# Gather passes of a graph layer: the second products of a block are issued behind the first products of the next block

## What is computed

```python
out = x @ root + bias
for r in range(8):
    mask = (edge_type == r)
    sums = segment_sum(x[src] * mask[:, None], dst, num_segments=1250)
    cnt  = segment_sum(mask, dst, num_segments=1250)
    out  = out + (sums / maximum(cnt, 1)[:, None]) @ weight[r]
```

## Time and profile before

| | us |
|---|---|
| median of 3 runs | 2362.14 (2356.88 to 2371.85) |
| the profiled execution | 2366.44 |
| span of its trace | 2364.7 |
| busy TensorE, matmuls | 2077.4 (88%) |
| busy VectorE | 1341.4 (57%) |
| busy ScalarE | 818.3 (35%) |
| busy GpSimd | 917.9 (39%) |
| the first and last product of the gather passes begin | 1064.5 and 1691.1 |

### The profile page before, as it was taken

The page is one execution under the profiler, slowest core; times in us unless marked ns, Lnnn a source line. Parts: engine busy times, 40 slices in busy tenths (PEclk is TensorE's granted clock), DMA queues, the critical chain, the costliest instruction groups (busy, mean ns, idle before and its releaser), DMA issues. The chain is left out here.

```text
span 2364.7 us, 27801 instructions
## 1 busy us (share of the span) xinstructions
PE 2077.4 (88%) x9485; PEld 1623.2 (69%) x9485; DVE 1341.4 (57%) x2374; ACT 818.3 (35%) x1068; POOL 917.9 (39%) x805
## 2 busy tenths in 40 slices
PE   7898988889999999969999999899799379999910
PEld 5676776667888888857767677677588258888810
DVE  7467667652222222209999998988798722222258
ACT  3111111112222222215555566666534123333311
POOL 0000045455555554007777777777300111000034
PEclk9999999999999999989999999999899789999965
DMA  5222265657777777559888898886355679875163
GB/s 172 83 71 71 88 210 180 207 181 258 261 262 254 247 251 265 210 161 319 302 295 293 285 331 292 306 297 230 102 179 174 260 233 332 299 291 211 45 246 118
DMA packets 159197, 524.55 MB, mean 222 GB/s; under 512 B 33578, under 2 KB 33962, under 8 KB 157024
## 3 DMA queue, kind: packets, MB, share of 16 engines
q1 hardware_dynamic: 84752, 313.16, 37.2%
q0 software_dynamic: 70432, 195.65, 25.5%
q10 hardware_dynamic: 3888, 14.16, 1.5%
HBM read 403.66 MB, written 148.94 MB: 234 GB/s over the span
## 5 line engine op out<-in xcount | busy, mean ns | idle before, releaser
L194 PE MATMUL psum<-w_hi,xnT_hi 128*128 128x512 f32 (+1 forms) x1600 | 440.8, 412 | 27.2 <-PEq L401 21.4
L194 PE MATMUL psum<-w_lo,xnT_hi 128*128 128x512 f32 (+1 forms) x1600 | 426.8, 397 | 0.0
L194 PE MATMUL psum<-w_hi,xnT_lo 128*128 128x512 f32 (+1 forms) x1600 | 414.9, 393 | 0.0
L792 POOL DMA_INDIRECT sorted_rows<-acc x313 | 332.9, 1064 | 116.4 <-issue 85.1
L194 PEld LDWEIGHTS psum<-w_hi,xnT_hi 128*128 128x128 f32 (+1 forms) x1600 | 305.2, 194 | 100.6 <-issue 24.7
L194 PEld LDWEIGHTS psum<-w_lo,xnT_hi 128*128 128x128 f32 (+1 forms) x1600 | 301.4, 188 | 75.0
L194 PEld LDWEIGHTS psum<-w_hi,xnT_lo 128*128 128x128 f32 (+1 forms) x1600 | 296.8, 186 | 73.5
L521 ACT ACTIVATE work<-psum 128x512 f32<-128x512 f32 (+1 forms) x150 | 89.9, 599 | 591.2 <-PE psum L194 527.7
L761 DVE TENSOR_TENSOR acc<-acc 128x1024 fp32r<-128x1024 f32 x64 | 78.5, 1227 | 380.0 <-DMA split_experts<-acc 259.3
L884 POOL DMA_INDIRECT w_lo<-y_rows,sort_row x176 | 232.9, 1324 | 92.1 <-issue 58.5
L884 POOL DMA_INDIRECT w_hi<-y_rows,sort_row x176 | 236.4, 1343 | 62.9 <-issue 53.2
(11 more groups left out here) (279 smaller groups left out, 2615.9 us busy)
## 6 DMA issues: line engine op xcount, KB each, us to landing
split_experts<-acc SPq DMA_DIRECT2D x128, 512.0 KB
ring<-split_experts SPq DMA_DIRECT2D x16, 4096.0 KB, 15.0
w_raw<-in_wchunks SPq DMA_DIRECT2D x88, 512.0 KB
y_rows<-work SPq DMA_DIRECT2D x144, 256.0 KB
acc<-in_wchunks SPq DMA_DIRECT2D x64, 512.0 KB
o_rows<-o_s ACTq DMA_DIRECT2D x27, 512.0 KB
work<-local_rows SPq DMA_DIRECT2D x26, 384.0 KB
acc<-in_bias SPq DMA_DIRECT2D x10, 512.0 KB, 9.7
```

What stands on the lines that cost most here:

```text
L194: i = pe.matmul(to[:rm, :], x_[:, k, m * P:m * P + rm], w_[:, s, k * HALF:(k + 1) * HALF], start=(n == 0), stop=(n == 3 * KD - 1))
L792: pool.indirect_dma_start(sorted_dram, IndirectOffsetOnAxis(ap=e_dest[:, c:c + 1], axis=0), e_rec[:, c, :], None, bounds_check=BLOCKS * P ...
```

## The change

TensorE's instructions are the same ones, in another order; no other engine's code changes. Before, a block had its hi products, three matmuls of the unit, then its lo products. Now a block has its hi products, then the lo products (or the direct products) **of the block before**, then three matmuls of the unit. Waits move with the instructions that they stand before: those for the flush and for `hot` of a new group still stand ahead of its first hi products, and now also ahead of the last products of the old group.

```diff
+                def first_part(j):
+                    n, g, k = SPLIT_NO[j], j // GROUP, j % GROUP
+                    pe.wait_ge(hi_done, n + 1)
+                    ...                                   # two hi products
+                    o.then_inc(hi_used, 1)
+
+                def last_part(j):
+                    b, g, k = j % SLOTS, j // GROUP, j % GROUP
+                    if direct(j):
+                        pe.wait_ge(landed[b], PLACED[b] + 16 * (j // SLOTS) + 16)
+                        pe.wait_ge(scaled_done, DIRECT_NO[j] + 1)
+                    else:
+                        pe.wait_ge(lo_done, SPLIT_NO[j] + 1)
+                    ...                                   # two direct or lo products
+                    o.then_inc(pe_done, 1)
...
-                        for j in range(GROUP * g, GROUP * (g + 1)):
-                            if direct(j):
-                                ...                       # three of the unit, then direct products
-                            else:
-                                ...                       # hi products, three of the unit, lo products
+                    for j in range(i * SLOTS, (i + 1) * SLOTS):
+                        g = j // GROUP
+                        if j % GROUP == 0:
+                            if g >= 2:
+                                pe.wait_ge(acc_done, ACC_NO[g - 2])
+                            pe.wait_ge(hot_done, g + 1)
+                        if not direct(j):
+                            first_part(j)
+                        if j >= 1:
+                            last_part(j - 1)
+                        for _ in itertools.islice(steps, 3 * KD // SLOTS):
+                            pass
+                last_part(BLOCKS - 1)
```

More of the change, by code:

```diff
@@ L986, in _ @@
                     pass
+                def first_part(j):
+                    n, g, k = SPLIT_NO[j], j // GROUP, j % GROUP
+                    pe.wait_ge(hi_done, n + 1)
+                    for q in range(2):
+                        o = pe.matmul(bank[2 * (g % 2) + q], hot[:, g % 2, k, :], y_hi[:, n % 2, q * HALF:(q + 1) * HALF],
+                                      start=k == 0, stop=False)
+                    o.then_inc(hi_used, 1)
[6 more added lines that the diff above has]
+                        pe.wait_ge(lo_done, SPLIT_NO[j] + 1)
+                    for q in range(2):
+                        at = slice(q * HALF, (q + 1) * HALF)
+                        if direct(j):
+                            o = pe.matmul(bank[2 * (g % 2) + q], hot_scaled[:, DIRECT_NO[j] % 2, :],
+                                          slot_of(b).bitcast(F32)[:, at], start=k == 0, stop=k == GROUP - 1)
+                        else:
+                            o = pe.matmul(bank[2 * (g % 2) + q], hot[:, g % 2, k, :], slot_of(b)[:, at],
+                                          start=False, stop=k == GROUP - 1)
+                    o.then_inc(pe_done, 1)
@@ L987, in _ @@
                 for i in range(PASSES):
                     steps = unit(UNIT_AT[i]) if i in UNIT_AT else iter(())
[L989 to L993, removed]
-                        for j in range(GROUP * g, GROUP * (g + 1)):
-                            b, k = j % SLOTS, j % GROUP
-                            first, last = k == 0, k == GROUP - 1
-                            if direct(j):
[L998 to L1004, removed]
-                            else:
[L1006 to L1018, removed]
```

## The result

| | before | changed |
|---|---|---|
| median, 8 runs each | 2363.35 (2356.88 to 2371.85) | 2382.18 (2377.88 to 2387.74) |
| profiled execution | 2366.44 | 2377.88 |
| span of its trace | 2364.7 | 2376.1 |

The ratio is 1.0073, with a 95% interval of 1.0054 to 1.0092: 13 to 22 us slower, some 17 by the ratio (the two medians of the table lie 18.8 apart), under the 1% that the prediction called no change. The forecast was 2373, its own range 2366 to 2381, the whole range 2360 to 2385. Direction and range held; the size was 11 us where some 17 came, and the median lies 1 us above the forecast's own range.

What follows compares the result with a forecast made beforehand. TensorE was taken to bound 39 passes at 13.88 us, VectorE the passes without a unit; 7.0 (longer loop in root passes) + 4.0 (passes behind those) = 11.0, 2362.1 + 11.0 = 2373 us; own range 2366 to 2381, whole 2360 to 2385.

Steps and rivals of the forecast that it cites:

- The bound and the loop: Passes with unit and root result: TensorE's 13.88 us gives way to a 14.32 loop, 0.44 longer; 16 x 0.44 = 7.0 us.
- 0.10 after its end. With 0.68 that is 0.78: Pass start: first hi products begin 0.10 us after `hot` ends, which takes 0.68, so 0.78 after its start.
- the cover of 0.35: Passes 22 to 30 and 33 to 41: loop without root result 13.53 us, under TensorE's 13.88, 0.35 to spare, no cost.
- every pass pays: Rival, chance 0.09: cover of 0.35 or the gathers' fails, 18 passes without root results pay too, 2381 to 2389 us.
- The passes behind those without a unit: Passes 10, 21, 32 and 43: direct products stand behind the wait, 4 x 1.0 = 4.0 us, between 0 and 9.8.
- (a): Passes 9, 20, 31, 42: TensorE's order is covered by VectorE's 15.82 of 16.59 us; costed at nothing.
- (b): Lo products and the slot's next gather come 0.47 us later; cover 1.45, costed at nothing.
- (c): Flush behind VectorE's fourth lo part: the direct products it needs are over earlier, cover over 3 us; costed at nothing.
- (d): Hi products released earlier give ScalarE a lead that a TensorE-bound pass can't use; costed at nothing.
- The wait did not dissolve: Rival, chance 0.14: VectorE runs ahead further, `hot` is ready in time at pass starts; 2362 us.
- The clock did not fall: Rival, chance 0.08: gaps in root passes bring half clock to half of some 17 passes, 24 plus 11: 2397 us.
- the 13.9 us: GpSimd contention with VectorE's lo parts: seven of 45 ns in 44 passes would be 13.9 us; left out.

Runs made afterwards that it cites:

- the first experiment: Changed order, but at a pass start the direct products come first again, ahead of the waits for the flush and `hot`: 2360.73 us, ratio 1.0002 to the kernel before.
- the dose of 0.14: Changed order with an extra 128x256 VectorE copy between flush and root result, once per pass with a root result: 2380.22 us, ratio 1.0084 to the kernel before.
- the second experiment: Old order, only the direct products moved behind the next pass's first hi products: 2398.86 us, ratio 1.0155 to the kernel before.
- the first kernel of the last experiment: Changed order with direct products first, one filling matmul per block and two more direct blocks in passes without a unit: 2356.23 us, ratio 0.997 to the kernel before.
- the third experiment: Changed order, but VectorE makes the next pass's first `hot` ahead of adding the root result: 2364.98 us, ratio 1.002 to the kernel before.

## Why the prediction was right, and where its sizes were off

**The bound and the loop held.** The kernel got slower through a longer loop at a pass start, with a cause that stands in one place: the first experiment removes it and loses nothing, the dose of 0.14 comes through as 0.14, the shortened link as 0.33. The signs named ahead were there: waits of 0.46 us ahead of the first hi products, VectorE over a microsecond for ScalarE before the fourth lo part (1.32), ScalarE for the second hi products (1.45), 13.82 to 13.89 in passes 22 to 30 and 33 to 41.

**The loop was mis-sized at two links of five,** by 0.16 and 0.07. Predicted, against the timeline above:

| link | predicted | measured |
|---|---|---|
| start of `hot` to first hi products | 0.78 | 0.94 |
| hi, direct products, unit | 2.88 | 2.95 |
| to the fourth lo part | 1.90 | 1.89 |
| lo part and flush | 1.20 + 1.13 | 1.20 + 1.14 |
| to the next `hot` | 6.43 | 6.43 |
| sum | 14.32 | 14.55 |

The first is the step "0.10 after its end. With 0.68 that is 0.78", which carried the gap of pass 9's second group over to the first group of a pass. Here the products begin 0.25 after the recorded end (1253.55 to 1253.80). The size of the matrix, 128x384 there and 128x512 here, is not the reason. In pass 2 of the changed kernel the same 128x512 matrix is followed after 0.1 us, and the link is the predicted one, 0.79. VectorE, then TensorE, for whose wait the row names no releaser:

```profile
1088.23 0.68 DVE L944 TENSOR_TENSOR hot<-lanes,sort_local 128x512 fp32r<-128x512 f32 x1
```

```profile
1089.02 0.70 PE L991 MATMUL psum<-y_hi,hot 128*128 128x512 f32 x2 [0.31 <-issue]
```

Passes 1 and 2 take 14.38 and 14.39 us, and only from pass 3 on is it 14.53 and more. With `hot` in two pieces the gap behind a piece of 128x128 is likewise 0.10 in passes 1 and 2 and 0.26 from pass 3 on. What the slow starts have in common stands in the code: from unit 4 on, which begins in pass 3, a unit has a wait of its own (for a result to have left its PSUM bank), and TensorE meets it right ahead of the group's waits. In the changed kernel every start on `hot` with that wait ahead comes after 0.25 to 0.26 (passes 3 to 8, 10, 12 to 19, 21, 32), and every one without it after 0.10 (passes 1, 2, 9, 20 and 43, and the second groups for which TensorE waited). The trace of before shows the same 0.25 at pass 21. No experiment moved this wait alone, and why it costs 0.15 is open. The second link is long by the 0.08 of a pair behind a gap: without a gap, in the experiment with the root result behind the next matrix, it took 2.87. Together 0.23 in each pass, so 0.67 instead of 0.44 over 13.88: 10.4 us measured in the 17 root passes with a unit against 7.0 for 16. Without a root result the loop is 14.55 - 0.79 = 13.76, so the cover of 0.35 was 0.12 and just held. The rival "every pass pays" was nearer than its 0.09 says; the second experiment shows the same passes at 14.23 once 0.47 more stands in the loop.

**The passes behind those without a unit** were put at 4.0 with bounds 0 to 9.8. Passes 10, 21 and 32 cost 6.7 and the end 1.5, so 8.2: within the bounds, double the term. Pass 21 alone costs 4.2, over its bound of 2.45. (The forecast's own range doesn't come out of the bounds either: 7.0 with 0 and with 9.8 gives 2369 to 2379, not 2366 to 2381.) The term took the 12.53 us of pass 21 as those of a pass at full clock. From `hot` to `hot` it was one, but the direct products just ahead ran mostly at half clock, 2.44 us recorded instead of 1.88. TensorE in the trace of before, and a window around their start (columns as in the earlier trace rows):

```profile
1363.79 2.44 PE L1003 MATMUL psum<-w_lo,hot_scaled 128*128 128x512 f32 x4
1366.42 0.70 PE L1009 MATMUL psum<-y_hi,hot 128*128 128x512 f32 x2 [0.19 <-DVE hot L944]
```

```profile
1359.00:1364.00 5.00, 4.36 (x9) 2.58 (x10) 4.79 (x6) 4.32 (x5) 3.13 (x2) 0.50 1.00 398
```

There they lie in time in which TensorE would have waited for `hot`, and cost nothing. TensorE, pass 21 of the changed kernel, and a window up to its first hi products:

```profile
1369.65 1.91 PE L1008 MATMUL psum<-w_lo,hot 128*128 128x512 f32 x4
1373.65 1.19 PE L991 MATMUL psum<-y_hi,hot 128*128 128x512 f32 x2 [2.09 <-DVE hot L944]
1374.64 3.62 PE L1005 MATMUL psum<-w_lo,hot_scaled 128*128 128x512 f32 x4
1377.27 2.27 PE L194 MATMUL psum<-w_hi,xnT_hi 128*128 128x512 f32 x3
1379.34 0.86 PE L991 MATMUL psum<-y_hi,hot 128*128 128x512 f32 x2
```

```profile
1365.00:1373.65 8.65, 5.85 (x13) 3.57 (x13) 7.95 (x10) 6.05 (x6) 4.26 (x4) 0.50 1.01 398
```

And VectorE's fourth lo part there:

```profile
1381.47 1.29 DVE L960 SCALAR_TENSOR_TENSOR w_hi<-w_hi,sort_recip,y_hi 128x1024 fp32r<-128x1024 f32 x1 [4.07 <-ACT y_hi L915]
```

TensorE idles 2.09 us for `hot`, then its direct products take 2.63 (1374.64 to 1377.27) instead of 1.31, and the unit's three 2.07 instead of 1.10 (behind direct products, 1255.65 to 1256.75): half clock, a granted clock of 0.79 as the pass's mean. The clock was at 0.50 before this wait too, as it was in the trace of before, where it had come back by 1365 us; here it comes back only at 1379. Such a stretch now lies in the loop, and VectorE passes it on as a wait of 4.07. The upper bound had the direct products at half clock; the unit behind them was left out of it. In eight kernels where the direct products stood ahead of the wait, in either order, pass 21 took 12.35 to 12.54; in the six where they stood behind it, 15.09 to 16.74. Among the eight it makes no difference whether the direct products run at half clock (2.48 us and 12.35 in the first experiment) or at full clock (1.31 us and 12.45 in the first kernel of the last experiment, which differs from it in other things too). What tips the clock is open: the filling matmuls took 1.6 off pass 21 but did not restore 12.35.

The old order's pass 10 was not steady either: 14.36 from `hot` to `hot` in the trace of before, at the low clock of the earlier trace rows, but 12.52 to 12.79 in the three experiments in the old order that left its direct products in place. So a single trace prices such a pass within about 2 us, no better, and the trace of before is the longest of the four in the old order from first `hot` to last flush (635.0 us against 630.0 to 633.4; the three others have each a small edit of their own). Against them the changed kernel's 653.1 is 20 to 23 us longer.

**The costs put at nothing.** (a) Passes 9, 20, 31 and 42: -0.3 in sum. (b) Gathers: ScalarE waited for slots 0 to 3 34 times and 44.4 us in the stage, against 11 times and 35.0 (26 of each being the stage's start), so the cover of 1.45 did fail, and for nothing: passes 22 to 30 stay at 13.86. (c) and (d) show no cost.

**The rivals.** The wait did not dissolve. The clock did not fall in the root passes: 1.00 from 1067 to 1189 with a gap in every pass. The Trainium skill (TensorE: Matmul & The Clock Gate, A second HAM failure mode: psum-queue depth-cycling) tells of frequent small idle times between groups of matmuls that made the clock swing; this trace does not show it for gaps of 0.46 us once in 14.55 us. GpSimd's contention with VectorE did not show: the lo parts over slots 0 to 3 in the changed kernel's stage take 1271 to 1341 ns with the median of before, 1283. The GPSIMD Engine Reference of the Trainium skill (Key points) would have had them longer if they now met more descriptor writing; leaving the 13.9 us out was right.

## What to carry to other kernels

In an in-order queue, work that is ready should stand ahead of a wait; behind it, it does not only lose its place as cover, it also delays whatever the waiting engines get from behind it. To price such a move, walk the loop from the late result to its next making, link by link, and compare its length with the bound engine's time for the pass: the difference is the loss per pass, and the total wait removed elsewhere says nothing about it. A reordering with two parts should be run as its two parts, since here one part was the whole loss and the other gave the loop 0.47 us back.

## What the runs showed of the hardware, not expected

- A wait more ahead of a group's first products goes with a later start: where TensorE stood waiting for the matrix, they begin 0.10 us after the recorded end of the matrix they wait for, and 0.25 where the unit's own wait stands right ahead of the group's, whatever the size of the matrix (128x128 to 128x512). That is 0.15 us in each root pass from pass 3 on.
- The first pair of matmuls behind a gap takes 0.54 us to the next start instead of 0.46 (1253.80 to 1254.34). The same 0.54 stands at the second group of a pass where the trace shows no gap. TensorE in pass 24 of the changed kernel:

```profile
1426.02 0.70 PE L991 MATMUL psum<-y_hi,hot 128*128 128x512 f32 x2
1426.56 0.63 PE L1008 MATMUL psum<-w_hi,hot 128*128 128x512 f32 x2
```

With `hot` in two pieces the passes with nothing else to wait for take 13.77 instead of 13.86 in the changed order, and that is this 0.54 going back to 0.46: the same pair begins at 1423.02 there and what follows at 1423.48. In the old order the pair falls to 0.47 as well, but the unit's three and the lo products behind it take 0.77 and 0.58 instead of 0.70 and 0.48, and the pass comes to 13.95. Why the pair is slow isn't settled.

- An instruction that waits for a result of its own engine can hide another at part of its price: the copy of 0.33 us cost the queue 0.14, since the root result behind it took 0.19 less of it (0.60 instead of 0.79). By the code it waits for the flush; behind `hot` instead of the flush, in the third experiment, it takes 0.60 too.
- Behind the waits of 3.06, 2.09 and 2.07 us at the starts of passes 10, 21 and 32 the matmuls ran at half clock (1.2 GHz) for some 3 to 6 us (5.69 in pass 21, 1373.65 to 1379.34), while 0.46 us in each pass of a row leaves the clock at 1.00. The waits alone are not shown to be the cause: at pass 21 the clock was low before, and in pass 9 of the kernel before it fell at 1201, TensorE's single idle times there being at most 1.13 us, and came back at 1211.
